# Second attention of a gated block: one sum per head and query in a column of 128, and the next tile's scores ahead of the spread

## The chip, the cores and the metric

The kernel runs on one core of a Trainium2 chip. The metric is device time in microseconds. The core has five engines with a queue of instructions each: TensorE (PE in the rows, its weight loads PEld), VectorE (DVE), ScalarE (ACT), GpSimd (POOL) and SyncE (SP). Within a queue instructions start in the order in which they are written; between queues they wait for semaphores.

## What is computed

The reference is a block of four stages over 8 batches of 128 rows by 256 columns: an attention to a context, a feed-forward with quantised weights, a second attention with 16 heads, and a second feed-forward. Each stage is gated and added to `x`. The change lies in the third stage:

```python
q, k, v = proj(hs, Wq, bq), proj(at, Wk, bk), proj(at, Wv, bv)     # 16 heads of 16 columns
scores = clip(einsum('bhsd,bhtd->bhst', q, k) / sqrt(16), -50, 50)
scores = clip(where(attend, scores, -10000.0), -50, 50)
probs = softmax(scores, axis=-1)
ctx = einsum('bhst,bhtd->bhsd', probs, v)
delta = rs * (ctx @ Wo.T + bo)
delta = layernorm(delta) * ln_gamma + ln_beta
x = x + tanh(g_xattn[1]) * delta
```

## The kernel before

All instructions are written by hand, one function per engine; their order in each queue is the order of the Python code. A tile is one batch (128 queries against 128 context rows); there are `NT` = 8. The four stages run one behind the other, but the queues overlap at the seams: while the third stage works on tile `t`, products and copies of the fourth (`xd_t`, `hi_d`, `norm_d`, `lo_d`) for tile `t - 3` stand in the same queues.

In the third stage every engine runs a function `step_c(t, p)`, where `p` is the parity of the tile and chooses one of two buffers. On TensorE step `t` holds, in this order: the queries of tile `t + 1` (`q`, L1311); for tile `t - 1` the sums of the heads (`head_sums`, L1354), the head values (`head_values`, L1368) and the spread (`spread_sums`, L1379); the scores of tile `t + 1` (`scores`, L1409); the transpose of the normalised tile `t + 2` (`xt_c`, L1173); for tile `t - 3` the transpose for the last stage (`xd_t`, L1396); and the output projection of tile `t - 1` (`delta`, L1387).

What passes between the engines, for a tile `u`:

- ACT copies the queries with bias into `QM` (L1030, four instructions), TensorE makes the scores into banks `PB[0]` to `PB[3]`, and ACT takes their exponentials into `PR` (L1088, four of 512 columns; `PR` is a view of `HBQ`). DVE clips them, which also sets the masked rows (L860).
- `head_sums` adds the 128 context rows of each head. A head's exponentials lie as context rows by query columns, so a product with a matrix `SEL`, which has ones in one column, gives the sums of a head over all queries as one row in bank `PB[7]`. Heads come four at a time, into four groups of 32 partitions. A group holds 32 rows; before the change 8 of them are used, since the 128 queries of a head are cut into two halves of 64 columns and each half has its own row. So 16 heads of 128 sums lie in 64 columns, and 32 products of 64 columns fill them.
- DVE takes the reciprocal `RD` of these columns (L845).
- `spread_sums` multiplies `RD` with 0/1 matrices `SPREAD` so that each head's reciprocals stand on the 16 rows of its values, in `PB[7]` from column 256. Four products: two halves of the columns by two halves of the queries.
- ACT copies the head values from `PB[6]` to `PV` (L1094); DVE multiplies them with the spread reciprocals into `OT` (L855, a view of `HB`, and right behind it the clipping of the next tile).
- `delta` multiplies `OT` with the output weights; DVE scales and takes the mean and variance of the row (L870 to L881, and those of an older tile's `X`, L530 to L538), and POOL and ACT finish the normalisation.

DVE's step holds, in order: `RD`, the normalisations (L554, L829), `OT`, the clipping of the next tile, the last stage's subtraction `lo_d` (L835), the scaled delta (L870), and the statistics. ACT's step holds the four copies of the queries, then L1099 and L1094, two exponentials, the copy of the transposed tile (`copy_ht`, L937), the last stage's `hi_d` (L1081), and two exponentials. After the last tile TensorE goes on with the fourth stage (`gate_up_d`, L1467; `down_d`, L1484), whose first products stand ahead of the last sums.

A product of two float32 tiles stands in the trace as two issues of TensorE; hence 64 rows of L1354 per tile for 32 products.

Of the kernel before, what the change touches and what calls it, by code (L numbers as in the profile page):

```python
# [26 lines left out]
P = 128  # L27
NT = 8
D = 256
DC = D // P  # L30
# [5 lines left out]
HD = D // NH  # L36
HB32 = 32
CT4 = P // HB32
HPC = P // HD
# [29 lines left out]
def live(u):  # L69

    return 0 <= u < NT
# [14 lines left out]
def gated_block(nc, x, ctx, ctx_t, mask_b, mask_i, scalars, w0_in, w3_0, wqkvo, bq, bk, bv, bo,  # L86
                gamma, beta, w1_in, wd_1, ident_in, heads_in, out):
    with ExitStack() as stack:
        def sb(name, shape, dt=F32):
            return stack.enter_context(nc.sbuf_tensor(name, shape, dt))  # L90
# [15 lines left out]
        ident = sb("ident", [P, P])  # L106
# [63 lines left out]
        HQL = sb("HQL", [P, FC, P], F32R)  # L170

        V1 = sb("V1", [P, 2, NH, HB32])
        SEL = sb("SEL", [P, 2 * CT4, HB32])
        SPREAD = sb("SPREAD", [P, 2 * DC, P])

        VA = CTX
        PAR = sb("PAR", [P, 2])
        BQM = sb("BQM", [P, DC, 2])
        PR = HBQ[:].rearrange("p (b a) n -> p b (a n)", b=2)
        RD = sb("RD", [P, P // 2])  # L180
        C_OUT = HB[:].rearrange("p b g s -> p (b g s)")[:, 0:6 * D].rearrange("p (k n) -> p k n",
                                                                              k=6)
        OT, DL, XD, PV, D1, D2 = (C_OUT[:, k, :] for k in range(6))
# [43 lines left out]
        def head_at(h):  # L227

            c, j, e = h // HPC, h % HPC // 2, h % 2
            return j * 4 * P + (2 * c + e) * P  # L230
# [88 lines left out]
        def _(pool):  # L319
# [7 lines left out]
            nc.gpsimd.memset(V1[:], 0.0).then_inc(set_pool, 1)  # L327
            nc.gpsimd.memset(SEL[:], 0.0).then_inc(set_pool, 1)
            pool.wait_ge(set_pool, 4)
            for r in range(2 * CT4):  # L330
                nc.gpsimd.memset(SEL[:, r, r:r + 1], 1.0).then_inc(set_pool, 1)
            nc.gpsimd.memset(SEL[:, 0, 2 * CT4:], 1.0).then_inc(set_pool, 1)

            def rstd(t, m):

# [27 lines left out]
                nc.gpsimd.tensor_tensor(NMB[:, t:t + 1], NMB[:, t:t + 1], RSTD[:, t:t + 1],  # L363
                                        ALU.mult).then_inc(nm_x, 1)

            def spread_rows(c, half):
                at = 4 * c + half
                rows = ident[:].rearrange("p (j s) -> p j s", s=HB32)[:, :, at:at + 3:2]
                nc.gpsimd.tensor_copy(
                    SPREAD[:, 2 * c + half, :].rearrange("p (j e d) -> p j e d", e=2, d=HD),  # L370
                    rows.unsqueeze(3).broadcast_to([P, CT4, 2, HD])).then_inc(set_spread, 1)

            x_groups = [P, D // GS, GS]
# [40 lines left out]
                step_a(t, t % 2)  # L414
            pool.wait_ge(ld["ident"], 16)
            for c in range(DC):
                for half in range(2):
                    spread_rows(c, half)


            def halves(buf, p, half):
# [104 lines left out]
        def _(dve):  # L526
# [313 lines left out]
            def step_c(t, p):  # L840
                if t == NT:
                    gu_d(0)
                if live(t - 1):
                    dve.wait_ge(c_dn, t)
                    nc.vector.reciprocal(RD[:], PB[7][:, 0:P // 2]).then_inc(c_rd, 1)  # L845
                if live(t + 2):
                    norm(t + 2, p, 2)
                if live(t - 3):
                    norm_d(t - 3)
                if t == NT:  # L850
                    lo_gu(0)
                if live(t - 1):
                    dve.wait_ge(c_sp, t)
                    dve.wait_ge(c_pc, t)
                    nc.vector.tensor_tensor(OT, PV, PB[7][:, D:2 * D], ALU.mult  # L855
                                            ).then_inc(c_o, 1)
                if live(t):

                    dve.wait_ge(c_ex, 4 * t + 4)
                    nc.vector.tensor_scalar(PR[:, p, :], PR[:, p, :], SC_HI[:, bass.ds(t, 1)],  # L860
                                            EXP_LO, ALU.min, ALU.max).then_inc(c_p, 1)
                if live(t - 3):
                    lo_d(t - 3)
                if t == NT:
                    stats(t - 2, p, t - 2 + 2 * NT)
                    gu_d(1)
                if live(t - 1):
                    dve.wait_ge(c_dl, t)
                    need(dve, c_d1, t - 1)
                    nc.vector.scalar_tensor_tensor(  # L870
                        out=DL, in0=PB[5][:, 0:D], scalar=RES[:], in1=BO[:],
                        op0=ALU.mult, op1=ALU.add).then_inc(c_de, 1)
                    dve.wait_ge(c_de, t)
                    nc.vector.bn_stats(ST2[:], DL).then_inc(c_st, 1)  # L874
                    dve.wait_ge(c_st, t)
                    nc.vector.bn_aggr(MV2[:], ST2[:]).then_inc(c_mv, 1)
                    dve.wait_ge(c_mv, t)
                    need(dve, c_of, t - 1)
                    nc.vector.tensor_scalar(NM2[:], MV2[:, 0:1], -1.0, None, ALU.mult
                                            ).then_inc(c_nm, 1)  # L880
                    nc.vector.tensor_scalar(VE2[:], MV2[:, 1:2], LN_EPS, None, ALU.add  # L881
                                            ).then_inc(c_ve, 1)
                if t == NT:
                    lo_gu(1)
                elif live(t - 2):
                    stats(t - 2, p, t - 2 + 2 * NT)
# [277 lines left out]
        def _(pe):  # L1164
# [1 line left out]
            for _ in range(WARMUPS):  # L1166
                nc.tensor.matmul(PB[7][:, 0:P], ONES[:], ONES[:], start=True, stop=True)
            pe.wait_ge(ld["ident"], 16)
            pe.wait_ge(set_pool, 2 * CT4 + 5)

            def transpose_x(src, bank, done):
                for c in range(DC):
# [172 lines left out]
            def head_sums(u, p):  # L1345

                pe.wait_ge(c_p, u + 1)
                for c in range(DC):
                    for e in range(2):
                        for half in range(2):  # L1350
                            r = (2 * c + e) * 2 + half
                            for j in range(CT4):
                                at = head_at(HPC * c + 2 * j + e) + half * (P // 2)
                                mm = nc.tensor.matmul(  # L1354
                                    PB[7][HB32 * j:HB32 * (j + 1), 0:P // 2], SEL[:, r, :],
                                    PR[:, p, at:at + P // 2], start=(r == 0),
                                    stop=(r == 2 * CT4 - 1))
                mm.then_inc(c_dn, 1)

            def head_values(u, p):  # L1360
                pe.wait_ge(c_v, 2 * u + 2)
                need(pe, c_pc, u)
                need(pe, d_hl, u - 2)
                for c in range(DC):
                    for e in range(2):
                        for j in range(CT4):
                            h = HPC * c + 2 * j + e
                            mm = nc.tensor.matmul(  # L1368
                                PB[6][HB32 * j:HB32 * (j + 1), c * P:(c + 1) * P],
                                V1[:, p, h, :], PR[:, p, head_at(h):head_at(h) + P],  # L1370
                                start=(e == 0), stop=(e == 1))
                mm.then_inc(c_pv, 1)

            def spread_sums(u):

                pe.wait_ge(c_rd, u + 1)
                for k in range(2 * DC):
                    at = D + k * (P // 2)
                    mm = nc.tensor.matmul(PB[7][:, at:at + P // 2], SPREAD[:, k, :], RD[:],  # L1379
                                          start=True, stop=True)  # L1380
                mm.then_inc(c_sp, 1)

            def delta(u):
# [16 lines left out]
            def scores(t, p):  # L1400


                for c in range(DC):
                    pe.wait_ge(c_qm, 4 * t + 2 * (c + 1))
                    for j in range(CT4):
                        rows = slice(HB32 * j, HB32 * (j + 1))
                        if c == 0:
                            need(pe, c_ex, 4 * t - 3 + j)
                        mm = nc.tensor.matmul(PB[j][:, 2 * c * P:2 * (c + 1) * P],  # L1409
                                              KTA[rows, t, c, :], QM[rows, p, c, :, :],  # L1410
                                              start=True, stop=True)
                        if c == DC - 1:
                            mm.then_inc(c_s, 1)

            def step_c(t, p):
                if live(t + 1):
                    q(t + 1, 1 - p)
                if t == 1:
                    pe.wait_ge(b_hl, 2 * NT)
                    pe.wait_ge(x_done, 2 * NT)  # L1420
                    pe.wait_ge(set_spread, 2 * DC)
                if t == NT:

                    pe.wait_ge(c_ex, 4 * NT)
                    gate_up_d(0)
                if live(t - 1):
                    head_sums(t - 1, 1 - p)
                    head_values(t - 1, 1 - p)
                if live(t - 1):
                    spread_sums(t - 1)  # L1430
                if live(t + 1):
                    scores(t + 1, 1 - p)
                if live(t + 2):
                    xt_c(t + 2, p)
                if live(t - 3):
                    xd_t(t - 3)
                if t == NT:
                    gate_up_d(1)
                if live(t - 1):
                    delta(t - 1)  # L1440
# [112 lines left out]
```

## Time and profile before

| what | value |
|---|---|
| median of three runs | 244.17 us (243.62 to 246.03) |
| the profiled execution | 244.73 us, its span 242.9 us |
| TensorE busy | 217.0 us (89% of the span) |
| VectorE, ScalarE, GpSimd busy | 155.4, 135.3 and 125.3 us |
| second attention, from the first sums to the last | 116.82 to about 168 us |

The profiled execution's own time holds 1.8 us around its span. All times in the rows count from the start of the span. TensorE's rows have modelled ends, since its products overlap; what one group costs is read from the start of one group to the start of the next. An idle time in brackets is that of the engine ahead of the instruction, with the instruction that ended it.

### The profile page before, as it was taken

The page shows a single profiled execution, that of the slowest core. Times are in us where ns is not written, and L with a number is a line of the kernel's source. Part 1 is how long each engine was busy: PE and PEld are TensorE (multiplying, and loading weights), DVE is VectorE, ACT ScalarE, POOL GpSimd, SP SyncE. Part 2 cuts the span into 40 slices and gives each one's busy share as a digit, 9 for nine tenths or more (in the row PEclk, how much of TensorE's full clock was granted, in tenths as well). Part 3 has the DMA queues.
Part 4 walks back from the last instruction along what each step waited for, and adds up shares of the span by engine and source line. Part 5 has one row for each costly group of instructions (what it writes and reads, how often), then busy time and mean ns, then how long its engine had stood idle before and what let it go on. Part 6 is the DMA issues. An engine that isn't in the chain of part 4 may idle for free. (4 is left out here: it accounts for less than half of the span.)

```text
span 242.9 us, 5228 instructions
## 1 busy us (share of the span) xinstructions
PE 217.0 (89%) x1960; PEld 176.7 (73%) x1960; DVE 155.4 (64%) x391; ACT 135.3 (56%) x288; POOL 125.3 (52%) x202
## 2 busy tenths in 40 slices
PE   8399997989999899866999999979989999999992
PEld 7266565768877687754878778767868888888872
DVE  1775788678899999826457777785563432444233
ACT  2132888687887788794667877544342322323230
POOL 3546363867887876645847777797379100000000
PEclk9959997999999999999999999979999999999999
DMA  4999203650000000000000000000000000020002
GB/s 137 366 400 369 60 3 88 258 173 3 0 1 0 3 1 0 3 0 0 3 3 5 3 4 3 3 3 0 3 0 0 3 1 0 0 89 0 0 0 86
DMA packets 9576, 12.59 MB, mean 52 GB/s; under 512 B 1104, under 2 KB 8016, under 8 KB 9552
## 3 DMA queue, kind: packets, MB, share of 16 engines
q1 hardware_dynamic: 9120, 12.07, 14.3%
q8 instruction: 15, 0.25, 0.4%
q10 hardware_dynamic: 432, 0.20, 0.4%
q14 instruction: 9, 0.07, 0.1%
HBM read 11.22 MB, written 1.05 MB: 50 GB/s over the span
## 5 line engine op out<-in xcount | busy, mean ns | idle before, releaser
L1467 PE MATMUL PB<-SGN,WHI 128*128 128x512 f32 x128 | 41.8, 408 | 0.0
L814 DVE TENSOR_TENSOR QM<-SIL,PB 128x512 f32<-128x512 f32 x16 | 11.0, 688 | 33.5 <-ACT SIL L1140 33.5
L1140 ACT ACTIVATE SIL<-PB 128x512 f32<-128x512 f32 x16 | 9.6, 599 | 36.4 <-PE PB L1467 36.4
L1467 PEld LDWEIGHTS PB<-SGN,WHI 128*128 128x128 f32 x128 | 23.9, 195 | 4.6
L1484 PE MATMUL PB<-WHI,SGN 128*128 128x256 f32 x128 | 25.7, 284 | 1.4 <-DVE SGN L822 1.4
L1270 PE MATMUL PB<-SGN,XQH 128*128 128x512 f32 x64 | 26.2, 409 | 0.0
L1467 PE MATMUL PB<-SGN,WLO 128*128 128x512 f32 x64 | 25.7, 402 | 0.0
L1270 PE MATMUL PB<-SGN,XQL 128*128 128x512 f32 x64 | 25.6, 400 | 0.0
L440 POOL TENSOR_TENSOR HBQ<-HB,HSD 128x512 f32<-128x512 f32 x16 | 16.7, 1045 | 15.4 <-ACT HB L1047 15.3
L1088 ACT ACTIVATE HBQ<-PB 128x512 f32<-128x512 f32 x32 | 17.5, 613 | 10.8 <-PE PB L1409 10.8
L337 POOL TENSOR_TENSOR RSTD<-MVS,MHALF 128x1 f32<-128x1 f32 x24 | 14.5, 605 | 16.3 <-DVE MVS L538 16.3
L1484 PEld LDWEIGHTS PB<-WHI,SGN 128*128 128x128 f32 x128 | 20.7, 188 | 2.2 <-DVE SGN L822 1.6
L1285 PE MATMUL PB<-SGN,HQH 128*128 128x256 f32 x64 | 17.3, 304 | 0.8 <-DVE HQL L722 0.8
L1484 PE MATMUL PB<-WLO,SGN 128*128 128x256 f32 x64 | 18.0, 281 | 0.0
L822 DVE TENSOR_TENSOR SGN<-QM,SGN 128x512 fp32r<-128x512 f32 x16 | 12.4, 775 | 7.9 <-ACT SGN L1144 7.9
L447 POOL TENSOR_TENSOR WLO<-WRAW,WHI 128x512 fp32r<-128x512 f32 (+1 forms) x16 | 17.3, 1110 | 0.0
L434 POOL TENSOR_TENSOR HB<-HB,HR 128x512 f32<-128x512 f32 x16 | 16.7, 1045 | 0.0
L1144 ACT CAST SGN<-QM 128x512 fp32r<-128x512 f32 x16 | 9.9, 619 | 11.6 <-DVE QM L814 11.6
L1285 PE MATMUL PB<-SGN,HQL 128*128 128x256 f32 x64 | 15.9, 281 | 0.0
L1038 ACT ACTIVATE SIL<-PB,WSC 128x512 f32<-128x512 f32 x16 | 11.0, 688 | 7.7 <-PE PB L1270 7.7
L1298 PE MATMUL PB<-ident,HBQ 128*128 128x128 f32 x64 | 10.3, 284 | 5.0 <-POOL HBQ L440 4.9
L722 DVE TENSOR_TENSOR HQL<-PB,HQH 128x512 fp32r<-128x512 f32 x16 | 10.8, 676 | 6.0 <-ACT HQH L1052 5.7
(140 smaller groups left out, 557.5 us busy)
## 6 DMA issues: line engine op xcount, KB each, us to landing
WRAW<-w_dram SPq DMA_DIRECT2D x3, 1024.0 KB, 10.9
WRAW<-w_dram SPq DMA_DIRECT2D x1, 2048.0 KB, 7.4
X<-x_dram SPq DMA_DIRECT2D x2, 512.0 KB, 7.0
CTXT<-ctxt_dram SPq DMA_DIRECT2D x2, 512.0 KB, 8.2
CTX<-ctx_dram SPq DMA_DIRECT2D x2, 512.0 KB, 9.2
WRAW<-wd_dram SPq DMA_DIRECT2D x1, 1024.0 KB, 5.6
out_dram<-X SPq DMA_DIRECT2D x4, 256.0 KB, 2.5
WQK<-wqkvo_dram SPq DMA_DIRECT2D x1, 512.0 KB, 10.8
```

The source lines that it names most:

```text
L337: nc.gpsimd.tensor_tensor(RSTD[:, bass.ds(t, 1)], MVS[:, bass.ds(t, 1), 1], MHALF[:], ALU.pow).then_inc(rstd_ready, 1)
L434: nc.gpsimd.tensor_tensor(h, h, spread(HR, p, half), ALU.mult).then_inc(b_v, 1)
L440: nc.gpsimd.tensor_tensor(halves(HQ, p, half), h_part(p, half), spread(HSD, p, half), ALU.mult).then_inc(b_hq, 1)
L447: nc.gpsimd.tensor_tensor(part(WLO), part(WRAW), part(WHI).bitcast(F32), ALU.subtract).then_inc(w_lo, 1)
L814: nc.vector.tensor_tensor(GU[:, b, :], SG[:, b, :], PB[2 * b + 1][:], ALU.mult).then_inc(d_g, 1)
L822: nc.vector.tensor_tensor(GUL[:, b, :], GU[:, b, :], GUH[:, b, :].bitcast(F32), ALU.subtract).then_inc(d_gl, 1)
L1038: nc.scalar.activation(SIL[:, half, :], PB[2 * half][:], ACT.Silu, scale=WSC[:, 0:1]).then_inc(b_sil, 1)
L1088: nc.scalar.activation(PR[:, p, b * 512:(b + 1) * 512], PB[b][:], ACT.Exp, scale=1.0 / math.sqrt(HD)).then_inc(c_ex, 1)
L1270: mm = nc.tensor.matmul(PB[2 * half + m][:], part[:, p, c, :], sgn(m, c, a, b), start=(c == 0 and k == 0), stop=(c == DC - 1 and k == 1))
L1285: mm = nc.tensor.matmul(PB[7][:, 0:D], part[:, j, :], sgn3(j), start=(j == 0 and i == 0), stop=(j == FC - 1 and i == 1))
L1467: mm = nc.tensor.matmul(PB[2 * b + m][:], wcol(w_part, m, c, j), act_part[:, c, g * TG:(g + 1) * TG], start=(c == 0 and i == 0), stop=(c = ...
L1484: mm = nc.tensor.matmul(down_bank(g, k), act_part[:, b, ts], wdown(w_part, j), start=(j == 0 and i == 0 and k % 2 == 0), stop=(j == FC - 1 ...
```

## The change

The queries of a head are no longer cut in two. `SEL` has four columns of ones in place of eight, so that of the 32 rows of a group 4 are used, and a head's 128 sums lie in 128 columns. The sums are 16 products of 128 columns, `RD` is a reciprocal of 128 columns, and the spread is two products of 128 columns. On TensorE the scores of the next tile are issued ahead of the spread. GpSimd sets up half as many columns of `SEL` and two tables `SPREAD` in place of four.

```diff
-        RD = sb("RD", [P, P // 2])
+        RD = sb("RD", [P, P])
...
-                    nc.vector.reciprocal(RD[:], PB[7][:, 0:P // 2]).then_inc(c_rd, 1)
+                    nc.vector.reciprocal(RD[:], PB[7][:, 0:P]).then_inc(c_rd, 1)
...
-                        for half in range(2):
-                            r = (2 * c + e) * 2 + half
-                            for j in range(CT4):
-                                at = head_at(HPC * c + 2 * j + e) + half * (P // 2)
-                                mm = nc.tensor.matmul(
-                                    PB[7][HB32 * j:HB32 * (j + 1), 0:P // 2], SEL[:, r, :],
-                                    PR[:, p, at:at + P // 2], start=(r == 0),
-                                    stop=(r == 2 * CT4 - 1))
+                        r = 2 * c + e
+                        for j in range(CT4):
+                            at = head_at(HPC * c + 2 * j + e)
+                            mm = nc.tensor.matmul(
+                                PB[7][HB32 * j:HB32 * (j + 1), 0:P], SEL[:, r, :],
+                                PR[:, p, at:at + P], start=(r == 0), stop=(r == CT4 - 1))
...
-                for k in range(2 * DC):
-                    at = D + k * (P // 2)
-                    mm = nc.tensor.matmul(PB[7][:, at:at + P // 2], SPREAD[:, k, :], RD[:],
-                                          start=True, stop=True)
+                for c in range(DC):
+                    mm = nc.tensor.matmul(PB[7][:, D + c * P:D + (c + 1) * P], SPREAD[:, c, :],
+                                          RD[:], start=True, stop=True)
...
-                if live(t - 1):
-                    spread_sums(t - 1)
                 if live(t + 1):
                     scores(t + 1, 1 - p)
+                if live(t - 1):
+                    spread_sums(t - 1)
```

On TensorE, in a step in the middle of the stage, before (L1311 queries, L1354 sums, L1368 head values, L1379 spread, L1409 scores, L1173 transpose; `x31` repeats the row above it; the wait `c_rd` is for `RD`, `c_qm` for the copies of the queries, `c_o` for `OT`):

```order
L1354 MATMUL PB<-HBQ,SEL 32x64 x31
L1368 MATMUL PB<-HBQ,V 32x128 [waits d_hl,c_pc,c_v]
L1368 MATMUL PB<-HBQ,V 32x128 x15
L1379 MATMUL PB<-RD,SPREAD 128x64 [waits c_rd]
L1379 MATMUL PB<-RD,SPREAD 128x64 x3
L1409 MATMUL PB<-QM,KTA 128x256 [waits c_ex,c_qm]
L1409 MATMUL PB<-QM,KTA 128x256 [waits c_ex] x3
L1409 MATMUL PB<-QM,KTA 128x256 [waits c_qm]
L1409 MATMUL PB<-QM,KTA 128x256 x3
L1173 MATMUL PB<-ident,XH 128x128 [waits c_qm,ln_done]
```

The same place after it; the line numbers are those of the changed kernel (L1404 scores, L1374 spread):

```order
L1351 MATMUL PB<-HBQ,SEL 32x128 x15
L1364 MATMUL PB<-HBQ,V 32x128 [waits d_hl,c_pc,c_v]
L1364 MATMUL PB<-HBQ,V 32x128 x15
L1404 MATMUL PB<-QM,KTA 128x256 [waits c_ex,c_qm]
L1404 MATMUL PB<-QM,KTA 128x256 [waits c_ex] x3
L1404 MATMUL PB<-QM,KTA 128x256 [waits c_qm]
L1404 MATMUL PB<-QM,KTA 128x256 x3
L1374 MATMUL PB<-RD,SPREAD 128x128 [waits c_rd]
L1374 MATMUL PB<-RD,SPREAD 128x128
L1171 MATMUL PB<-ident,XH 128x128 [waits c_qm,ln_done]
```

Eight products of the scores have moved ahead of the wait for `RD`, and the spread has half as many products of twice the columns.

On TensorE at the end of the stage, after the change, where no scores are left (the sums of tile 6, and then the first products of the fourth stage; L1391 is `xd_t`, L1382 delta, L1462 `gate_up_d`):

```order
L1351 MATMUL PB<-HBQ,SEL 32x128 x15
L1364 MATMUL PB<-HBQ,V 32x128 [waits d_hl,c_pc,c_v]
L1364 MATMUL PB<-HBQ,V 32x128 x15
L1374 MATMUL PB<-RD,SPREAD 128x128 [waits c_rd]
L1374 MATMUL PB<-RD,SPREAD 128x128
L1391 MATMUL PB<-ident,HB 128x128 [waits d_hl,c_pc,d_ln]
L1391 MATMUL PB<-ident,HB 128x128
L1382 MATMUL PB<-WQK,HB 128x256 [waits c_de,c_o]
L1382 MATMUL PB<-WQK,HB 128x256
L1462 MATMUL PB<-SGN,WHI 128x512 [waits d_hl,w_lo,c_ex]
```

Here the order is that of before; only the columns of the sums and of the spread differ. The order on the other engines is unchanged.

## Rows read from the trace of the kernel before

**Rows 1.** Stretches: length, busy PE, PEld, DVE, ACT, POOL (instructions), granted clock, DMA.
```profile
123.41:130.00 6.59, 6.40 (x135) 5.21 (x134) 3.78 (x10) 4.60 (x11) 4.58 (x7) 1.00 0.00 0
...
136.60:143.46 6.86, 6.66 (x138) 5.43 (x137) 5.11 (x14) 4.98 (x13) 5.12 (x8) 1.00 0.01 2
...
150.32:155.84 5.52, 5.32 (x128) 4.25 (x127) 4.08 (x11) 3.64 (x10) 4.37 (x8) 1.00 0.02 3
```

**Rows 2.** Timeline of TensorE in one step: start, us, instruction, count, [idle before, releaser].
```profile
123.41 1.10 PE L1354 MATMUL PB<-HBQ,SEL 128*32 128x64 f32 x64
124.33 1.06 PE L1368 MATMUL PB<-HBQ,V 128*32 128x128 f32 x32
125.32 1.10 PE L1379 MATMUL PB<-RD,SPREAD 128*128 128x64 f32 x8
126.35 1.15 PE L1409 MATMUL PB<-QM,KTA 32*128 32x256 f32 x16
...
127.70 1.03 PE L1387 MATMUL PB<-WQK,HB 128*128 128x256 f32 x4
128.92 1.16 PE L1311 MATMUL PB<-HT,WQK 128*128 128x128 f32 x8 [0.19 <-ACT HT L937]
```

**Rows 3.** Timeline of the other engines and the weight loads in that step.
```profile
123.57 1.51 ACT L1030 ACTIVATE QM<-PB,BQM,PAR 128x128 f32<-128x128 f32 x4 [0.31 <-issue]
...
124.58 0.56 DVE L845 RECIPROCAL RD<-PB 128x64 f32<-128x64 f32 x1 [0.99 <-PE PB L1354]
...
126.46 0.42 DVE L855 TENSOR_TENSOR HB<-HB,PB 128x256 f32<-128x256 f32 x1 [1.09 <-PE PB L1379]
...
127.43 0.20 PEld L1173 LDWEIGHTS PB<-ident,XH 128*128 128x128 f32 x2 [0.33 <-issue]
...
127.51 1.09 ACT L1088 ACTIVATE HBQ<-PB 128x512 f32<-128x512 f32 x2 [1.69 <-PE PB L1409]
...
128.49 0.38 ACT L937 COPY HT<-PB 128x256 f32<-128x256 f32 x1
```

**Rows 4.** Chain of waits in a long step: start, us, what.
```profile
145.63 1.10 PE PB L1379 x8
146.73 1.08 PE PB L1409 x16
```

**Rows 5.** Timeline of VectorE in the long step before it and in it.
```profile
142.63 0.42 DVE L835 TENSOR_TENSOR SGN<-PB,SGN 128x256 fp32r<-128x256 f32 x1 [1.03 <-ACT SGN L1081]
...
145.03 0.55 DVE L845 RECIPROCAL RD<-PB 128x64 f32<-128x64 f32 x1
...
145.95 0.41 DVE L829 TENSOR_SCALAR HB<-X,MVS,RSTD 128x256 f32<-128x256 f32 x1
...
147.11 1.34 DVE L860 TENSOR_SCALAR HBQ<-HBQ,SC_HI 128x2048 f32<-128x2048 f32 x1
```

**Rows 6.** Groups by line, shapes apart: the reciprocals; busy us, mean ns, idle before.
```profile
L845 DVE RECIPROCAL RD<-PB 128x64 f32<-128x64 f32 x8 | 4.4, 552 | 5.2 <-PE PB L1354 5.2
...
L710 DVE RECIPROCAL HR<-HSD 128x8 f32<-128x8 f32 x16 | 3.3, 203 | 0.3
```

**Rows 7.** Timeline of the last step before the final stage.
```profile
160.22 0.42 DVE L855 TENSOR_TENSOR HB<-HB,PB 128x256 f32<-128x256 f32 x1 [0.48 <-PE PB L1379]
...
160.56 1.65 DVE L860 TENSOR_SCALAR HBQ<-HBQ,SC_HI 128x2048 f32<-128x2048 f32 x1
...
160.70 1.34 PE L1387 MATMUL PB<-WQK,HB 128*128 128x256 f32 x4 [0.29 <-DVE HB L855]
```

**Rows 8.** Chain of waits behind it: start, us, what.
```profile
162.04 4.16 PE PB L1467 x12
...
169.87 2.80 PE PB L1467 x12
...
172.67 0.86 PE PB L1387 x4
```

**Rows 9.** Busy time by stretch there; columns as in Rows 1.
```profile
162.00:163.00 1.00, 1.00 (x4) 0.81 (x3) 0.97 (x4) 0.32 (x2) 1.00 (x2) 0.50 0.00 0
```

More of the change, by code:

```diff
@@ L172, in gated_block @@
         V1 = sb("V1", [P, 2, NH, HB32])
-        SEL = sb("SEL", [P, 2 * CT4, HB32])
-        SPREAD = sb("SPREAD", [P, 2 * DC, P])
+        SEL = sb("SEL", [P, CT4, HB32])
+        SPREAD = sb("SPREAD", [P, DC, P])
         VA = CTX
@@ L329, in _ @@
             pool.wait_ge(set_pool, 4)
-            for r in range(2 * CT4):
+            for r in range(CT4):
                 nc.gpsimd.memset(SEL[:, r, r:r + 1], 1.0).then_inc(set_pool, 1)
-            nc.gpsimd.memset(SEL[:, 0, 2 * CT4:], 1.0).then_inc(set_pool, 1)
+            nc.gpsimd.memset(SEL[:, 0, CT4:], 1.0).then_inc(set_pool, 1)
             def rstd(t, m):
@@ L364, in x_offset, with spread_rows @@
                                         ALU.mult).then_inc(nm_x, 1)
-            def spread_rows(c, half):
-                at = 4 * c + half
-                rows = ident[:].rearrange("p (j s) -> p j s", s=HB32)[:, :, at:at + 3:2]
+            def spread_rows(c):
+                rows = ident[:].rearrange("p (j s) -> p j s", s=HB32)[:, :, 2 * c:2 * c + 2]
                 nc.gpsimd.tensor_copy(
-                    SPREAD[:, 2 * c + half, :].rearrange("p (j e d) -> p j e d", e=2, d=HD),
+                    SPREAD[:, c, :].rearrange("p (j e d) -> p j e d", e=2, d=HD),
                     rows.unsqueeze(3).broadcast_to([P, CT4, 2, HD])).then_inc(set_spread, 1)
@@ L416, in _ @@
             for c in range(DC):
-                for half in range(2):
-                    spread_rows(c, half)
+                spread_rows(c)
             def halves(buf, p, half):
@@ L1168, in _ @@
             pe.wait_ge(ld["ident"], 16)
-            pe.wait_ge(set_pool, 2 * CT4 + 5)
+            pe.wait_ge(set_pool, CT4 + 5)
             def transpose_x(src, bank, done):
@@ L1349, in head_sums @@
                     for e in range(2):
-                        for half in range(2):
-                            r = (2 * c + e) * 2 + half
-                            for j in range(CT4):
-                                at = head_at(HPC * c + 2 * j + e) + half * (P // 2)
-                                mm = nc.tensor.matmul(
-                                    PB[7][HB32 * j:HB32 * (j + 1), 0:P // 2], SEL[:, r, :],
-                                    PR[:, p, at:at + P // 2], start=(r == 0),
-                                    stop=(r == 2 * CT4 - 1))
+                        r = 2 * c + e
[4 more added lines that the diff above has]
+                                PR[:, p, at:at + P], start=(r == 0), stop=(r == CT4 - 1))
                 mm.then_inc(c_dn, 1)
@@ L1420, in step_c @@
                     pe.wait_ge(x_done, 2 * NT)
-                    pe.wait_ge(set_spread, 2 * DC)
+                    pe.wait_ge(set_spread, DC)
                 if t == NT:
@@ L1428, in step_c @@
                     head_values(t - 1, 1 - p)
+                if live(t + 1):
+                    scores(t + 1, 1 - p)
                 if live(t - 1):
                     spread_sums(t - 1)
-                if live(t + 1):
-                    scores(t + 1, 1 - p)
                 if live(t + 2):
```

## The prediction, made before the changed kernel ran

> **What bounds the kernel now.** I read the stretches first, cut at the starts of successive sums of the heads [rows 1]. A step of the second attention takes 6.59 us at first (three steps, from the sums at 116.82, 123.41 and 130.00), 6.86 us where products of the last stage stand in the queues too (two steps, 136.60 and 143.46), and 5.52 us in the one without a next projection of queries (150.32). TensorE is busy for all but 0.2 us of each, so a reader would say that TensorE bounds it. The timeline of one step shows the order of its work [rows 2]: sums 123.41, head values 124.33, spread 125.32, scores 126.35, then the transpose, delta 127.70, and the queries 128.92. The other engines show what ties them together [rows 3]: the reciprocal RD runs beside the head values, the product OT waits 1.09 us for the spread, the exponentials wait 1.69 us for the scores, and the copy of the transposed tile stands behind two exponentials on ACT, so that the queries wait for it, 0.19.
>
> The chain of waits says that the 6.86 us steps are something else [rows 4]: RD, spread, scores, transposes, delta, then DVE's queue and back to RD. There TensorE waits for RD, and the scores lie inside the loop although nothing that RD needs comes from them. DVE's rows give that queue [rows 5].
>
> **The change part by part.** All times below count from the start of the sums of a tile.
>
> *Sums.* 64 issues of 64 columns become 32 of 128. Head values are 32 issues of exactly that shape; from first start to last end they take 1.06 us, the sums 1.10 [rows 2]. So 0.92 becomes 0.88: the columns streamed are the same.
>
> *Reciprocal.* 64 columns take 552 ns, 8 take 203 [rows 6]: 6.2 ns a column, so 128 take 0.95 us, 0.40 more. Bounds: nothing more, and 1.10 (twice the whole of it); I take the slope, since both rows are the same operation. The Trainium skill, "VectorE: DVE Perf Modes", section "First, the fixed hardware budget", says that a reciprocal repeats its divide steps 8 times, and its section "Specifications" gives the engine 0.96 GHz; as an estimate from that page, 64 columns more would cost 0.53 us, and the sum below would end near 240.2. It speaks against the change, and the two rows here do not bear it out.
>
> *Spread.* Four products become two, eight issues four. The eight take 1.03 us to the next group [rows 2]; a product of 128 columns over the full array costs the same, since the queries' eight issues of 128 take 1.08 (128.92 to 130.00) [rows 1, 2]. So four take 0.52 to 0.54. OT starts 1.14 us after the spread does [rows 2, 3]; it will be 0.62.
>
> *Order.* Scores stand ahead of the spread. Sums, head values (0.99, any wait for RD included), scores (1.08) [rows 2, 4] put the spread at 0.88 + 0.99 + 1.08 = 2.95. RD starts 1.17 after the sums where DVE is free [rows 3] and ends at 2.1: covered with 0.8 us to spare. OT follows at 2.95 + 0.62 = 3.57, which is later than now (3.05). That is new: delta waits for OT, 0.48 after its start (160.22 to 160.70) [rows 7], so it starts at 4.05; TensorE has only the transposes to do meanwhile and stands for about 0.3 us. Delta takes 0.86 [rows 8], queries 1.08: next sums at 3.57 + 0.48 + 0.86 + 1.08 = 5.99.
>
> Other work must fit in 5.99. The copy of the transposed tile: exponentials start 1.16 after the scores, the copy 0.98 later for 0.38 [rows 2, 3], hence 1.87 + 2.52 = 4.39, before the queries want it at 4.91: that wait goes. The four copies of the queries end at 125.08 (123.57 + 1.51) [rows 3], 2.75 after the queries begin (1.08 before the sums at 123.41); the second half of the scores now wants them at 1.08 + 0.88 + 0.99 + 0.54 = 3.49. What is queued behind that wait would be the spread, so OT, clipping and next sums: 0.7 us of room. Clipping: 0.34 behind OT and 1.34 long [rows 5, 7], so 5.25, before the sums at 5.99; at 1.65 it would still fit. POOL is busy 5.12 us of a long step [rows 1].
>
> *DVE in the long steps.* From the last-stage subtraction to RD 2.40 (142.63 to 145.03), RD to the last-stage normalisation 0.92, now 1.32, that 0.41, OT 0.34, clipping 1.34 [rows 5, 7]: 5.81 in all. Thus it fits by 0.18. In phase: clipping ends at 5.25 - 5.99 = -0.74, RD starts at 1.66 and ends at 2.61, before the spread's place at 2.95. So the long steps lose both the scores from the loop and the spread's half, and become 5.99 as well.
>
> *The end.* The step at 150.32 has no transpose and no queries behind it. OT of its tile at 3.57; clipping done at 5.25; DVE runs its 2.40 to RD, 0.95, and 0.04 + 0.62 to the next OT: 9.26 against 9.90 now (150.32 to 160.22) [rows 1, 7]. Here no scores remain to hide RD, so its 0.40 eats most of the spread's 0.52. The last sums meet the same exchange: 0.1 gained.
>
> *Setup.* POOL does two copies and four small fills less; it has waits behind both, so nothing.
>
> **Sum.** Three short steps 3 x (6.59 - 5.99) = 1.80; two long ones 2 x (6.86 - 5.99) = 1.74; the end 0.64 + 0.1. Together 4.28. The profiled execution took 244.73 us (242.9 of it span): 240.45. It was 0.56 above the median of the three runs; from the median, 244.17 - 4.28 = **239.9**.
>
> **The rivals.**
> *DVE becomes the loop.* Its margin is 0.18 us, and clipping took 1.34 in a long step but 1.65 in the last [rows 7]. Then a long step is 5.81 + 0.31 = 6.12, or 6.25 with a reciprocal at twice the row. That costs at most 0.26 twice and some 0.45 at the end, 1.0 in all: 240.9. For it: DVE's idle time in the long steps nearly vanishes. Against it: the long steps' own clipping row is the short one.
> *The head values and the scores don't follow each other freely.* The first use 32 columns of the array, the second 32 rows, and nowhere in the trace does one follow the other directly. After the scores the weight loads of the next full product stood 0.33 us [rows 3]. If that comes once more in six steps, 2.0 us go: 241.9. Against it: 0.99 for the head values already contains such an end.
> *The half clock at the end goes, or comes twice.* At 162 us the granted clock is 0.50 [rows 9], the 1.2 GHz level, after TensorE stood for RD and then for OT; twelve products take 4.16 instead of 2.80 [rows 8]. The change leaves both stands and lengthens them slightly, so I keep the loss. Without it 239.9 - 1.4 = 238.5; with another like it 241.3.
> *Slower: the clock falls inside the steps.* The new stand before delta comes in every step, and if TensorE then ran at the lower level in a stretch of each, every stretch would cost about 1.4 us; four of them outweigh the 4.28 and six (one a step) give 239.9 + 8.4 = 248.3. Against it: TensorE already stands 0.2 us in each step, and the granted clock is 1.00 in all of them [rows 1].
>
> **How the numbers follow.** Forecast 239.9 with chance 0.58; DVE's loop 0.14; the free following fails 0.12; the clock at the end otherwise 0.12; slower 0.04. The low end takes the clock's gain and a little of the runs' own scatter (243.62 to 246.03): 238.2. The high end takes the second rival: 242.0. A change of under 1% (2.4 us) is about what a measurement of this kernel can't tell from none; faster by more than that means under 241.7. The forecast, DVE's loop, 0.10 of the clock's 0.12 and 0.04 of the second rival's 0.12 fall there: 0.86; the rest of those two, 0.10, lies within 1%; slower by more 0.04.
>
> **What would show it.** In the new profile: RD at 0.95 us; four issues of spread beginning as the scores end, with no wait for RD before them in the six steps; equal steps of about 6.0 us from 117 to 147; exponentials waiting less, and the copy of the transposed tile no longer named before the queries; a small wait of delta for OT in every step. I am wrong if RD is named before the spread in the long steps (DVE's loop), if the scores start more than 1.0 after the head values (second rival), or if the steps stay above 6.4. The exchange of RD against spread alone, without the order, should be worth little: what carries the forecast is that the scores fill RD's time.

## The result, and the profile after

| | before | after |
|---|---|---|
| median of 20 executions each | 245.09 us (243.50 to 249.03) | 242.44 us (239.69 to 244.01) |
| the profiled execution | 244.73 us, span 242.9 us | 242.91 us, span 241.1 us |
| first sums of the stage to the last | 116.82 to 166.12, 49.30 us | 118.28 to 164.32, 46.04 us |
| from the last sums to the end of the span | 76.78 us | 76.78 us |

The stage is measured here from the start of its first sums to the start of its last; the "about 168 us" that stands ahead of the prediction is where the last spread starts (168.13).

The ratio of after to before is 0.9881, with a 95% interval of 0.9847 to 0.9914. The change makes the kernel faster by about 2.9 us (245.09 x 0.0119); the medians, which hold disturbed executions that the ratio leaves out, differ by 2.65. The forecast was a gain of 4.28 us, and its range ended at 242.0: the side is right, and the gain is smaller than forecast.

The busy time by stretch, cut again at the starts of successive sums: length, busy PE, PEld, DVE, ACT, POOL with their instructions, granted clock, DMA. The first three rows answer to [rows 1], the fourth to [rows 9].

```profile
124.41:130.55 6.14, 5.84 (x99) 4.83 (x99) 4.15 (x10) 4.60 (x11) 4.73 (x7) 1.00 0.01 3
136.69:142.82 6.13, 6.13 (x101) 5.03 (x100) 5.94 (x15) 4.96 (x12) 4.83 (x9) 1.00 0.01 4
148.96:154.42 5.46, 5.06 (x92) 3.78 (x91) 4.85 (x14) 4.62 (x11) 4.15 (x8) 1.00 0.01 3
...
162.00:163.00 1.00, 1.00 (x4) 0.81 (x3) 0.72 (x4) 0.00 (x0) 1.00 (x3) 0.50 0.00 0
```

All five full steps are now equal, 6.13 to 6.14 us, where they were 6.59 three times and 6.86 twice; 5.99 was forecast. DVE is busy for 5.94 us of the long one, so it is nearly full. The half clock behind the stage is still there.

TensorE's timeline of a step, after, with the same columns as [rows 2]:

```profile
124.41 1.08 PE L1351 MATMUL PB<-HBQ,SEL 128*32 128x128 f32 x32
125.31 1.06 PE L1364 MATMUL PB<-HBQ,V 128*32 128x128 f32 x32
126.30 1.15 PE L1404 MATMUL PB<-QM,KTA 32*128 32x256 f32 x16
127.37 0.71 PE L1374 MATMUL PB<-RD,SPREAD 128*128 128x128 f32 x4
127.92 0.38 PE L1171 MATMUL PB<-ident,XH 128*128 128x128 f32 x2
128.60 1.13 PE L1382 MATMUL PB<-WQK,HB 128*128 128x256 f32 x4 [0.29 <-DVE HB L853]
129.57 1.05 PE L1309 MATMUL PB<-HT,WQK 128*128 128x128 f32 x8
130.55 1.08 PE L1351 MATMUL PB<-HBQ,SEL 128*32 128x128 f32 x32
```

The other engines and the weight loads in that step, after, answering to [rows 3]:

```profile
125.56 0.96 DVE L843 RECIPROCAL RD<-PB 128x128 f32<-128x128 f32 x1 [0.52 <-PE PB L1351]
...
128.12 0.42 DVE L853 TENSOR_TENSOR HB<-HB,PB 128x256 f32<-128x256 f32 x1 [1.37 <-PE PB L1374]
...
127.46 1.08 ACT L1086 ACTIVATE HBQ<-PB 128x512 f32<-128x512 f32 x2 [0.63 <-PE PB L1404]
128.43 0.38 ACT L935 COPY HT<-PB 128x256 f32<-128x256 f32 x1
...
127.37 0.52 PEld L1374 LDWEIGHTS PB<-RD,SPREAD 128*128 128x128 f32 x4 [0.33 <-issue]
```

RD ends at 126.52, the spread follows the scores at 127.37 and waits for nothing. The copy of the transposed tile ends at 128.81, ahead of the queries at 129.57. The one new stand is delta's, 0.29 us for OT.

A long step, after, on TensorE and VectorE, answering to [rows 4, 5]; the first line of VectorE is the clipping of the step before it:

```profile
138.57 1.15 PE L1404 MATMUL PB<-QM,KTA 32*128 32x256 f32 x16
139.65 0.71 PE L1374 MATMUL PB<-RD,SPREAD 128*128 128x128 f32 x4
...
134.60 1.71 DVE L858 TENSOR_SCALAR HBQ<-HBQ,SC_HI 128x2048 f32<-128x2048 f32 x1
...
138.62 0.95 DVE L843 RECIPROCAL RD<-PB 128x128 f32<-128x128 f32 x1
...
140.40 0.42 DVE L853 TENSOR_TENSOR HB<-HB,PB 128x256 f32<-128x256 f32 x1
140.74 1.34 DVE L858 TENSOR_SCALAR HBQ<-HBQ,SC_HI 128x2048 f32<-128x2048 f32 x1
```

RD ends at 139.57, 0.08 us before the spread: just in time. VectorE has no idle time ahead of OT either. The loop of [rows 4] is broken, and the chain of waits through this step names TensorE's groups alone.

The end of the stage on both engines, after, answering to [rows 7], and then the chain of waits behind it, answering to [rows 8]:

```profile
157.67 0.71 PE L1374 MATMUL PB<-RD,SPREAD 128*128 128x128 f32 x4 [1.30 <-DVE RD L843]
...
158.89 1.41 PE L1382 MATMUL PB<-WQK,HB 128*128 128x256 f32 x4 [0.29 <-DVE HB L853]
...
158.42 0.42 DVE L853 TENSOR_TENSOR HB<-HB,PB 128x256 f32<-128x256 f32 x1 [0.49 <-PE PB L1374]
```

```profile
160.31 4.10 PE PB L1462 x12
...
168.06 2.80 PE PB L1462 x12
170.86 0.86 PE PB L1382 x4
```

From the sums at 148.96 to this OT it is 9.46 us, against 9.90 before and 9.26 forecast.

**Why the span gained less than the stage.** The stage is 3.26 us shorter, the profiled span 1.8, since the first sums of this execution start 1.46 us later. One stretch ahead of the stage differs most, that of the first loads; the busy time there before, with the columns of [rows 1]:

```profile
8.00:20.00 12.00, 9.52 (x37) 6.59 (x37) 7.77 (x30) 3.37 (x13) 7.21 (x9) 0.72 1.07 387
```

And the same stretch after:

```profile
8.00:20.00 12.00, 9.38 (x29) 6.83 (x30) 8.17 (x30) 3.40 (x12) 6.37 (x6) 0.57 1.06 385
```

The granted clock there was 0.57 instead of 0.72, which is 1.8 us of full speed (12 x 0.15) at most. This differs between executions, whatever the kernel: in the ten profiles of this study the first sums start between 115.99 and 121.48. The experiment with the first part of the last stage's products moved has the setup of after, starts at 116.90, and its clock in this stretch was 0.86: so the changed setup does not delay it every time. That it never does isn't shown: the two profiles with the setup of before start at 116.82 and 115.99, earlier than all eight with the changed one. Executions of the same mean granted clock (0.983 to 0.984) took 242.86 us on average before (six) and 239.74 after (three): 3.12 us, close to the stage's 3.26.

### The profile page after: what moved, and what is told of

Its sections match the earlier page's. It is cut to its first block, busy times and chain, and to the rows that moved or that the text cites. A ratio compares the mean times of both kernels' runs of the same rounds, so it can differ in the third digit from the quotient of the medians.

```text
span 241.1 us, 4646 instructions
## 1 busy us (share of the span) xinstructions
PE 215.2 (89%) x1672; PEld 175.3 (73%) x1672; DVE 159.3 (66%) x391; ACT 135.3 (56%) x288; POOL 125.0 (52%) x196
## 4 chain that ended last, share of the span: by engine, by line
PE 43%; DVE 5%; issue 1%; ACT 1%; DVEq 0%; ACTq 0%
PE PB L1462 19%; PE PB L1479 8%; PE PB L1382 3%; PE PB L1404 3%; PE PB L1351 3%; PE PB L1309 2%; PE PB L1374 2%; PE PB L1364 2%; DVE HB L853 1%; ACT SIL L1138 1%; DVE RD L843 1%; DVE HB L827 1%; PE PB L1391 1%; DVE X L897 1%; DVE QM L812 0%
## 5 line engine op out<-in xcount | busy, mean ns | idle before, releaser
L1462 PE MATMUL PB<-SGN,WHI 128*128 128x512 f32 x128 | 41.7, 408 | 0.0
L1462 PEld LDWEIGHTS PB<-SGN,WHI 128*128 128x128 f32 x128 | 24.0, 195 | 4.6
L1462 PE MATMUL PB<-SGN,WLO 128*128 128x512 f32 x64 | 25.7, 402 | 0.0
L820 DVE TENSOR_TENSOR SGN<-QM,SGN 128x512 fp32r<-128x512 f32 x16 | 12.9, 806 | 7.9 <-ACT SGN L1142 7.9
L1028 ACT ACTIVATE QM<-PB,BQM,PAR 128x128 f32<-128x128 f32 x32 | 12.0, 457 | 7.0 <-issue 4.3
```

The source lines that it names most:

```text
L820: nc.vector.tensor_tensor(GUL[:, b, :], GU[:, b, :], GUH[:, b, :].bitcast(F32), ALU.subtract).then_inc(d_gl, 1)
L1028: nc.scalar.activation(QM[:, t % 2, c, e, :], PB[4][:, D + c * P:D + (c + 1) * P], ACT.Identity, bias=BQM[:, c, e:e + 1], scale=PAR[:, e:e ...
L1462: mm = nc.tensor.matmul(PB[2 * b + m][:], wcol(w_part, m, c, j), act_part[:, c, g * TG:(g + 1) * TG], start=(c == 0 and i == 0), stop=(c = ...
```

## The experiments

Each experiment also names the lengths between successive sums of the heads, from the first to the last: before they are 6.59, 6.59, 6.60, 6.86, 6.86, 5.52 and 10.28, after 6.13, 6.14, 6.14, 6.13, 6.14, 5.46 and 9.90. The first theory is the prediction's: the scores fill RD's time, and the spread's half is gained because of that. The rivals are that one of the two edits does it alone, and that DVE's queue decides.

**The changed kernel again.** No edit.

> The changed kernel again, to compare the stretches of two profiles of it. Theory: the stage itself takes the same time in each execution (sums of tile 0 to sums of tile 7 in 46.0 us, steps of 6.14 us, against 49.30 and 6.59 to 6.86 before), and what differs between executions lies ahead of it, in the first 45 us, where the first load lands and where TensorE's granted clock is 0.50 for a while; the start of the first sums (116.8 before, 118.3 after) will be another one than 118.3 by up to 1.5 us. Rival: the change itself, by its shorter setup on GpSimd, moves the first stage; then the first sums start at 118.3 again, within 0.2.

The median was 242.11 us and the ratio 0.9904 (0.9863 to 0.9945). The stage is the same to 0.02 us (46.06), with first sums at 118.89. What the profile says of the stage holds from one execution to another.

**The order alone.**

```diff
-                if live(t - 1):
-                    spread_sums(t - 1)
                 if live(t + 1):
                     scores(t + 1, 1 - p)
+                if live(t - 1):
+                    spread_sums(t - 1)
```

This is made in the kernel before, so that sums, RD and spread stay as they were.

> Order of the change alone, sums in 64 columns as before. Theory, both parts are needed: a step is sums 0.92, head values 0.99, scores 1.08, spread to OT 1.14, OT to delta 0.48, delta 0.97, queries 0.98, in all 6.56 us in short and long steps alike; so 0.03 is gained in each short step, 0.3 in each long one, nothing at the end: 0.7 us in all, ratio 0.997. Rival, the order carries the gain by itself: steps of 6.1 to 6.2 us and 3.0 us or more gained, ratio 0.988.

The ratio was 0.9970 (0.9929 to 1.0012). The five steps are 6.55 us each, then 5.85 and 8.34. TensorE and VectorE in a step of this kernel:

```profile
125.52 1.10 PE L1379 MATMUL PB<-RD,SPREAD 128*128 128x64 f32 x8
126.46 0.39 PE L1173 MATMUL PB<-ident,XH 128*128 128x128 f32 x2
127.14 1.13 PE L1387 MATMUL PB<-WQK,HB 128*128 128x256 f32 x4 [0.29 <-DVE HB L855]
128.10 1.05 PE L1311 MATMUL PB<-HT,WQK 128*128 128x128 f32 x8
...
126.66 0.42 DVE L855 TENSOR_TENSOR HB<-HB,PB 128x256 f32<-128x256 f32 x1 [2.16 <-PE PB L1379]
```

The long steps lose their loop (6.86 to 6.55), the short ones nearly nothing: the eight issues of the spread now stand right ahead of delta, which waits for OT. From spread to OT is 1.14 us, wherever the eight issues stand.

**The sums in 128 columns alone.**

```diff
-                if live(t + 1):
-                    scores(t + 1, 1 - p)
                 if live(t - 1):
                     spread_sums(t - 1)
+                if live(t + 1):
+                    scores(t + 1, 1 - p)
```

This is made in the changed kernel, which puts the order of before back.

> Sums in 128 columns, two spread products and the longer reciprocal alone, the spread ahead of the scores as before. Theory: short steps about 6.4 us (the reciprocal's 0.40 stands open ahead of the spread, the spread gives back 0.39, and the scores start 0.2 earlier or later at most), long steps 6.85 as before since the loop through RD gains and loses the same; 0.3 to 0.8 us gained, ratio 0.997 to 0.999. Rival, the smaller number of products carries the gain: steps 0.4 us shorter everywhere and 2.5 us gained, ratio 0.990.

The ratio was 0.9951 (0.9909 to 0.9993). The steps are 6.46, 6.46, 6.45, 6.87, 6.88, then 5.52 and 8.73. The spread in a short step, with its OT, and in a long one:

```profile
127.51 0.71 PE L1374 MATMUL PB<-RD,SPREAD 128*128 128x128 f32 x4 [0.21 <-DVE RD L843]
...
128.26 0.42 DVE L853 TENSOR_TENSOR HB<-HB,PB 128x256 f32<-128x256 f32 x1 [0.57 <-PE PB L1374]
...
140.84 0.71 PE L1374 MATMUL PB<-RD,SPREAD 128*128 128x128 f32 x4 [0.62 <-DVE RD L843]
```

The longer RD stands open here: TensorE waits 0.21 us for it in a short step and 0.62 in a long one, which eats part of what the shorter spread gives back, and all of it in the long steps.

Put together, and without the 1.56 us that the half clock costs behind the stage (it did not come in these two profiles; its price is measured next), the stage is 0.80 us shorter with the order alone (49.30 - 46.94 - 1.56), 0.37 with the sums alone (49.30 - 47.37 - 1.56), and 3.26 with both. So 2.1 us come only when the scores cover RD and the spread is short at once.

**The half clock behind the stage: products that fill the stands.** This adds products of ones, whose result nobody reads, where TensorE stands for RD and for OT at the end.

```diff
+                if t == NT - 1:
+                    for _ in range(5):
+                        nc.tensor.matmul(PB[4][:, 0:P], ONES[:], ONES[:], start=True, stop=True)
                 if live(t - 1):
                     spread_sums(t - 1)
...
+                if t == NT - 1:
+                    nc.tensor.matmul(PB[4][:, 0:P], ONES[:], ONES[:], start=True, stop=True)
                 if live(t - 1):
                     delta(t - 1)
```

> The changed kernel with six products more that nobody reads, five while TensorE stands for RD of tile 6 and one while it stands for OT behind it. Theory, the granted clock falls at the end of the stage because TensorE stands there twice: the clock stays 1.00, the twelve first products of the last stage take 2.80 us instead of 4.10, and sums of tile 6 to sums of tile 7 take 8.4 us instead of 9.9, about 1.4 us less than the changed kernel. Rival, the clock falls for another reason, or the stands left elsewhere suffice: the twelve products take 4.1 us still and the time is that of the changed kernel within 0.4.

And the same kernel once more:

> The six unread products again, since the clock at the end had not fallen in two other kernels either that have the stands (the order alone, the sums alone). Theory, the filled stands keep the clock: 1.00 from sums of tile 6 to sums of tile 7 and 8.34 us between them again. Rival, the fall goes by where the execution stands and the products have nothing to do with it: the clock falls there in this execution, about 9.7 us.

Both profiles have 8.34 us between the last two sums, against 9.90; the ratios were 0.9837 (0.9765 to 0.9910) and 0.9812 (0.9764 to 0.9859). The end of the stage in the second:

```profile
156.47 1.38 PE L1428 MATMUL PB<-ONES 128*128 128x128 f32 x10
157.85 0.71 PE L1374 MATMUL PB<-RD,SPREAD 128*128 128x128 f32 x4
...
159.07 1.13 PE L1382 MATMUL PB<-WQK,HB 128*128 128x256 f32 x4
```

The spread comes 3.26 us after its sums (154.59 to 157.85), as in the changed kernel (3.25, 154.42 to 157.67): the filler hides nothing and delays nothing, and the 1.56 us is the clock alone. That the stands bring the fall isn't shown by it, though, nor that the products kept the clock. In the profile of the sums alone, TensorE's timeline has a longer stand:

```profile
161.17 0.71 PE L1374 MATMUL PB<-RD,SPREAD 128*128 128x128 f32 x4 [1.69 <-DVE RD L843]
```

And the busy time behind it there has the clock whole:

```profile
163.00:164.00 1.00, 1.00 (x6) 0.86 (x5) 1.00 (x2) 0.99 (x2) 1.00 (x1) 1.00 0.00 0
```

There is also a rival that these runs leave open. In both profiles with the products, and in that of the sums alone, the clock had already fallen once shortly ahead of the stage, and in the profile of the changed kernel it had not. The busy time of the same microsecond in the changed kernel, with the products (second profile), and with the sums alone:

```profile
110.00:111.00 1.00, 0.52 (x5) 0.32 (x3) 0.46 (x1) 0.79 (x3) 0.00 (x0) 1.00 0.00 0
```

```profile
110.00:111.00 1.00, 0.68 (x4) 0.41 (x3) 0.97 (x3) 0.09 (x1) 0.00 (x0) 0.50 0.00 0
```

```profile
110.00:111.00 1.00, 0.54 (x4) 0.24 (x2) 0.80 (x2) 0.44 (x2) 0.00 (x0) 0.50 0.00 0
```

So the products, or that earlier fall, may go with the whole clock at the end; no run here has the products without the earlier fall.

**Work in place of the stand: the first part of the last stage's products, 12 of them, issued between the head values and the spread of tile 6.**

```diff
-                if t == NT:
-                    pe.wait_ge(c_ex, 4 * NT)
-                    gate_up_d(0)
...
+                if t == NT - 1:
+                    pe.wait_ge(c_ex, 4 * NT)
+                    gate_up_d(0)
                 if live(t - 1):
                     spread_sums(t - 1)
```

> The changed kernel with the first twelve products of the last stage moved one step ahead, between the head values and the spread of tile 6, where TensorE stands 1.30 us for RD. Theory: at the end of the stage DVE's queue sets the time and TensorE's first products can lie beside it; the wait for RD of tile 6 goes, the sums of tile 7 start 7.5 us after those of tile 6 instead of 9.9, held by the clipping of tile 7, and RD of tile 7 comes about 1.5 us earlier; about 1.9 us less than the changed kernel where its clock falls there, 0.6 where it does not. Rival: the spread of tile 6 comes 1.4 us later for it and all that hangs on it too (OT, clipping, delta), so that only the fallen clock's share is gained or nothing.

The ratio was 0.9895 (0.9841 to 0.9950). Between the last two sums it is 7.98 us, 1.92 less than after; 1.56 of that is the clock, which is whole in this stretch, and 0.36 the moved work (8.34 - 7.98). Then the gain is given back: from the first sums to the end of the span it is 123.60 us against 122.82. TensorE's timeline of this kernel:

```profile
161.04 1.08 PE L1351 MATMUL PB<-HBQ,SEL 128*32 128x128 f32 x32 [0.95 <-DVE HBQ L858]
161.93 1.06 PE L1364 MATMUL PB<-HBQ,V 128*32 128x128 f32 x32
164.89 1.07 PE L1374 MATMUL PB<-RD,SPREAD 128*128 128x128 f32 x4 [1.90 <-DVE RD L843]
```

And its busy time behind that:

```profile
165.00:168.00 3.00, 3.00 (x10) 2.47 (x11) 2.10 (x7) 1.14 (x4) 2.95 (x3) 0.51 0.00 0
```

With the products gone from ahead of the last sums, TensorE stands 0.95 us for the clipping of their tile and 1.90 for the last RD, and the half clock comes there, at 165 to 168 us; in the changed kernel it lies at 160 to 163.

**The second part moved as well**, `gate_up_d(1)`, from behind `xd_t` to ahead of the last spread:

```diff
+                if t == NT:
+                    gate_up_d(1)
                 if live(t - 1):
                     spread_sums(t - 1)
...
-                if t == NT:
-                    gate_up_d(1)
```

> As the run before, and the next twelve products ahead of the spread of tile 7 too. Theory: the second stand, for RD of tile 7, is covered as well; delta of tile 7 about 3 us earlier than in the changed kernel, where 1.3 of it is the clock; 239.3 us against 242.3. Rival: the output of tile 7 is late for the last stage then and the gain comes back as a wait there; the time of the run before.

The median was 241.59 us and the ratio 0.9788 (0.9728 to 0.9848), the lowest of all; its interval and that of the changed kernel (0.9847 to 0.9914) only touch. The busy time of its last two stretches, from the sums at 157.63 to the last delta, has the clock at 1.00 throughout:

```profile
157.63:165.62 7.99, 6.73 (x86) 5.31 (x87) 5.93 (x14) 3.16 (x6) 7.17 (x10) 1.00 0.01 2
165.62:171.51 5.89, 5.60 (x82) 4.63 (x82) 4.96 (x14) 2.62 (x7) 4.39 (x7) 1.00 0.00 0
```

The last delta (171.51) comes 13.88 us after the sums at 157.63; after, it is 16.28 (154.42 to 170.70). That is 2.40 us less, where 3 was expected: the last sums still wait 0.97 us for clipping. Against the kernel with the unread products, whose clock is whole there too (14.72 us, 154.59 to 169.31), it is 0.84 less: that is the moved work, and the rest is the clock. In this profile too the clock had fallen ahead of the stage, at 112 us, so that the moved work kept it whole isn't shown. From the first sums to the end of the span it is 120.02 us against 122.82.

**The reciprocal twice.** This adds a second reciprocal of the same sums ahead of RD, into a buffer that nobody reads.

```diff
                     dve.wait_ge(c_dn, t)
+                    nc.vector.reciprocal(RD2[:], PB[7][:, 0:P])
                     nc.vector.reciprocal(RD[:], PB[7][:, 0:P]).then_inc(c_rd, 1)
```

> The changed kernel with a second reciprocal of the same 128 columns ahead of RD, its result unused: the suspected cost doubled. Theory, RD is covered by head values and scores, by 0.8 us in the short steps and by 0.1 in the long ones: short steps stay within 0.2 of 6.14, long steps become 6.9 to 7.1, and the end is 1.9 us longer; 3.5 to 4.0 us more than the changed kernel. Rival, RD lies on the loop everywhere: every step 0.95 longer and 6.6 us or more.

The ratio was 1.0255 (1.0188 to 1.0321). The steps are 6.14, 6.15, 7.03, 7.21, 7.20, then 5.88 and 10.74. TensorE and VectorE in a long step:

```profile
141.57 0.71 PE L1376 MATMUL PB<-RD,SPREAD 128*128 128x128 f32 x4 [0.42 <-DVE RD L845]
...
139.76 0.95 DVE L844 RECIPROCAL RD<-PB 128x128 f32<-128x128 f32 x1
140.63 0.89 DVE L845 RECIPROCAL RD<-PB 128x128 f32<-128x128 f32 x1
```

In two short steps 0.87 us more on DVE costs nothing: the scores cover it. In the other three, where work of the last stage stands in DVE's queue, each costs 0.9 to 1.1 us, as DVE becomes the loop. To the end of the span it cost 6.9 us, where 3.5 to 4.0 were expected. The five steps cost 3.05, and about 2 at most was expected (3.5 to 4.0 less 1.9 for the end): the third step, which was counted as a short one, went from 6.14 to 7.03 against the expectation, and the two long ones passed the expected 7.1. The rest is 0.42 in the next step and 0.84 at the end of the stage, less than the 1.9 expected there, and 2.57 behind the last sums, where the last RD comes later and a second fall of the clock shows (0.53 in 176 to 178 us).

## Why the prediction was right in its side and wrong in its size

Of the 4.28 us forecast the stage gave 3.26. The forecast's terms were 1.80 + 1.74 in the five full steps, 0.64 at the end and 0.1 behind it; measured are 2.82 (1.37 in three short steps, 1.45 in two long ones), 0.44 and 0.

*Sums, head values, scores.* Forecast 0.88, 0.99 and 1.08, measured 0.90, 0.99 and 1.07. Right. That the products of 32 columns and of 32 rows would not follow each other freely, a rival, did not come.

*Reciprocal.* Forecast 0.95, measured 0.947 to 0.957. The slope between the two rows held: 0.40 us for 64 columns. The estimate of 0.53 that was worked out from the Trainium skill's page "VectorE: DVE Perf Modes" (sections "First, the fixed hardware budget" and "Specifications") is decided against by the measurement here.

*Spread to OT: the step that failed.* Forecast 0.62, half of what it was before; measured 0.75, in the changed kernel and with the sums alone. From spread to transposes it is 0.94 us for eight issues (order alone) and 0.55 for four, which is 0.39 less and not half; OT starts 0.20 us after the transposes in both. Taking 1.14 for eight and 0.75 for four, an issue costs 0.10 and a fixed 0.36 stays. The forecast took off 0.52, half of the 1.03 from the spread to the next group, and so halved a part of the fixed share too. On each of the five steps it costs 0.13 of the 0.15 missing (6.14 - 5.99), because delta, which follows OT by 0.47 to 0.48 in short and long steps, is on the path, as I had it.

*Delta and queries.* The row that I took delta from is of the last stage, where it takes 0.86 [rows 8]; in a step it takes 0.97, with other work behind it. Queries take 0.98 instead of 1.08. The two misses cancel, 1.95 against 1.94.

*The long steps.* The mechanism was right: the spread doesn't wait for RD, the scores are out of the loop, and long steps equal short ones. The margin in the first of them was 0.08 us rather than the forecast's 0.34 (2.61 to 2.95 after the sums; measured 2.88 and 2.96). The forecast took 1.34 us for the clipping; ahead of this step it took 1.71. Ahead of the second long step it took 1.34 again, and RD ended 0.45 before the spread. In the step at 148.96, behind a clipping of 1.77, RD ended at 151.91 and the spread came 1.11 us after the scores instead of 1.07. So *DVE becomes the loop* was closer than I said, and its sign came without it: DVE's idle time is nearly gone (busy 5.94 of 6.13 us), but the step's length is TensorE's. The doubled reciprocal shows it coming when 0.87 us are added.

*The end.* Forecast 9.26, measured 9.46. The spread of 0.75 stands in it twice, once for each tile's OT (0.26 more), clipping took less. The half clock stayed, as forecast, and none came in the steps (1.00 in the rows above). The 0.1 behind the last sums did not come: that stretch is 76.78 us in both.

*The sum.* In the stage 1.02 us is missing: 0.72 in the steps, 0.20 at the end, 0.10 behind. The time missed by more than that, 242.44 against 239.9: 245.09, the median of 20, is 0.92 above the median of three on which the forecast stands, and 0.6 more lies within the ratio's interval, which takes in the stage's 3.26 (245.09 x 0.0086 to 245.09 x 0.0153, 2.11 to 3.75). The part ahead of the stage, which I took as fixed, moves by several microseconds from one execution to the next, and the high end of the range, 242.0, left no room for it.

*What was said of its parts* held in half: the sums alone are indeed worth little, 0.37 us, but so is the order, 0.80. Neither carries the forecast; the pair does.

## What to carry to other kernels

When one edit lengthens a step on one engine and another edit gives that step cover, price them together: here they are worth 0.80 and 0.37 us apart and 3.26 together. When the instructions of a group are halved, don't halve the time to the start of the next group: a part of it belongs to the group as a whole. Here half of 1.03 us promised 0.52, and 0.39 came off. With one count of instructions on record, half of that time is a bound; the size comes from two counts of the same group. Take a duration from the same stage as the step it is used for, and set a gain of one per cent against the spread of a part of the kernel that the change doesn't touch.

## What the runs showed of the hardware that was not expected

The half clock behind the stage is not told by the length of the stand ahead of it. It came in before, in after (twice) and with the doubled reciprocal, behind stands for RD of 1.30 us in after and 2.12 with the reciprocal; it stayed away with the sums alone, behind 1.69, and with the order alone, behind 0.89. With products in the stands it stayed away twice. What goes with it better is an earlier fall, at 109 to 116 us, ahead of the stage: five of the ten profiles have it (the sums alone, both with the unread products, both parts moved, the doubled reciprocal), and in four of these the clock stays whole at the end; of the five without it four fall there (before, after twice, the first part moved), and only the order alone does not. That is seen in ten executions and not tested. What decides is left open; its price, 1.56 us, is not.

The granted clock during the first loads, 8 to 20 us, differs between executions (0.72 before, 0.57 after, 0.86 with the first part moved), and with it the start of this stage.
